# The norms of two phases applied by VectorE instead of ScalarE, with a new order of steps and a new table of banks

## The reference

```python
x = L0(x, ctx)    # rotary q and k; softmax attention over 256 keys; out projection; + x
def L1(x, c):     # mod = silu(c) @ ada_w + ada_b  -> shift, scale, gate for each half
    x0, x1 = x[:, :128], x[:, 128:]
    x0 = x0 + gate * mha(ln(x0) * (1 + scale) + shift)      # phase 1: each half attends to itself
    x1 = x1 + gate * mha(ln(x1) * (1 + scale) + shift)
    ...                                                     # phase 2: each half attends to the other
    ...                                                     # MLP: gelu(mod(ln(x)) @ fc1) @ fc2, gated
x = L2(x, ctx)    # phase 3: attention, + query, layer norm with gamma and beta
x = L3(x, ctx)    # phase 4: layer norm, attention with weights quantised to three values, + residual

def ln(x):
    mu = mean(x); var = mean((x - mu) ** 2)
    return (x - mu) / sqrt(var + eps)
```

## Time and profile before

| | |
|---|---|
| median of 3 runs | 300.79 us (299.94 to 304.99) |
| the profiled execution, own time | 301.38 us |
| its span, first to last instruction | 299.6 us |
| busy: TensorE, VectorE, ScalarE, GpSimd | 260.2, 241.9, 235.4, 173.8 us |
| mean granted TensorE clock | 0.978 of full speed |

### The profile page before, as it was taken

The page is one execution under the profiler, slowest core; times in us unless marked ns, Lnnn a source line. Parts: engine busy times, 40 slices in busy tenths (PEclk is TensorE's granted clock), DMA queues, the critical chain, the costliest instruction groups (busy, mean ns, idle before and its releaser), DMA issues.

```text
span 299.6 us, 8817 instructions
## 1 busy us (share of the span) xinstructions
PE 260.2 (87%) x3104; PEld 158.4 (53%) x3104; DVE 241.9 (81%) x561; ACT 235.4 (79%) x522; POOL 173.8 (58%) x274
## 2 busy tenths in 40 slices
PE   4275987899898888998888999999989999999983
PEld 3263543455565666666656766575444545445542
DVE  4179998999487897798889388998999999998912
ACT  1232456799998786598899998998989899898991
POOL 7778759347796667665482878856455654620000
PEclk9999799999999997899999999999999999999997
DMA  6678654211232232133231213212221213030001
GB/s 175 202 190 214 153 163 118 64 49 46 64 91 58 75 98 73 49 83 89 72 89 28 72 40 80 73 36 59 55 68 42 74 51 80 22 102 26 21 3 35
DMA packets 40619, 23.81 MB, mean 79 GB/s; under 512 B 4856, under 2 KB 39680, under 8 KB 40448
## 3 DMA queue, kind: packets, MB, share of 16 engines
q1 hardware_dynamic: 37264, 19.30, 24.7%
q10 hardware_dynamic: 3056, 3.83, 4.8%
q0 software_dynamic: 256, 0.13, 0.2%
HBM read 6.64 MB, written 0.54 MB: 24 GB/s over the span
## 4 chain that ended last, share of the span: by engine, by line
PE 45%; DVE 21%; DMA 9%; ACT 8%; SPq 7%; issue 7%; ACTq 1%; POOL 1%; DVEq 0%; POOLq 0%
PE ps L700 27%; DVE neg_max L1111 14%; PE ps_heads L700 13%; SPq L493 6%; DMA q_stack<-q_parts 5%; ACT probs L925 3%; DMA q_stack<-max_rows 2%; PE ps L875 2%; DMA rope_rows<-in_rope,pos_row 1%; PE ps L879 1%; SPq L574 1%; DVE stats L1071 1%; DMA pos_i<-in_pos 1%; ACTq L493 1%; ACT hidden L1043 1%
## 5 line engine op out<-in xcount | busy, mean ns | idle before, releaser
L1111 DVE TENSOR_REDUCE neg_max<-ps 128x2 f32<-128x512 f32 (+1 forms) x256 | 158.6, 682 | 9.4 <-PE ps L700 8.8
L925 ACT ACTIVATE probs<-ps 128x512 f32<-128x512 f32 x256 | 134.8, 626 | 10.4 <-PE ps L700 9.8
L700 PE MATMUL ps_heads<-probs,v_cols 128*32 128x256 f32 (+1 forms) x1280 | 76.9, 348 | 2.5 <-ACT probs L925 1.5
L700 PE MATMUL ps<-k_stack,q_stack 62*128 62x256 bf16 (+1 forms) x640 | 66.0, 255 | 5.9 <-DMA q_stack<-q_parts 5.1
L700 PE MATMUL ps<-q_stack,k_stack 64*128 64x256 bf16 (+1 forms) x640 | 66.0, 254 | 1.8 <-DMA q_stack<-max_rows 1.4
L700 PEld LDWEIGHTS ps<-k_stack,q_stack 62*128 62x128 bf16 x640 | 33.1, 96 | 28.1 <-issue 7.9
L700 PEld LDWEIGHTS ps<-q_stack,k_stack 64*128 64x128 bf16 x640 | 33.6, 96 | 24.3 <-issue 8.8
L700 PEld LDWEIGHTS ps_heads<-probs,v_cols 128*32 128x32 f32 x1280 | 31.9, 110 | 26.5 <-issue 11.1
L676 POOL TENSOR_TENSOR rstd<-var_eps,minus_half 128x2 f32<-128x2 f32 x20 | 14.1, 705 | 37.3 <-DVE var_eps L1077 37.3
L700 PE MATMUL ps<-src_t,w 128*128 128x256 f32 x96 | 29.6, 425 | 2.2 <-issue 1.1
L476 POOL TENSOR_TENSOR k_parts<-q_f,k_parts 128x256 bf16<-128x256 f32 x20 | 13.4, 669 | 28.6 <-issue 25.0
(11 more groups left out here) (117 smaller groups left out, 381.8 us busy)
## 6 DMA issues: line engine op xcount, KB each, us to landing
k_stack<-k_parts SPq DMA_DIRECT2D x120, 64.0 KB, 2.1
q_stack<-q_parts SPq DMA_DIRECT2D x114, 64.0 KB, 2.1
w<-in_w ACTq DMA_DIRECT2D x3, 512.0 KB, 5.0
gates<-gate_row SPq DMA_DIRECT2D x1, 1536.0 KB, 6.7
rows<-in_rows ACTq DMA_DIRECT2D x1, 704.0 KB, 4.8
w<-in_w ACTq DMA_DIRECT2D x1, 576.0 KB, 5.0
q_stack<-max_rows SPq DMA_DIRECT2D x36, 8.0 KB
ctx_t<-in_ctx_t SPq DMA_DIRECT2D x4, 128.0 KB, 2.5
```

Source lines behind the costliest of these rows:

```text
L700: return nc.tensor.matmul(out, lhs_t, rhs, start=start, stop=stop, **k)
L925: nc.scalar.activation(probs[:, n % PROB_BUFS, :], ps[bank[st]][:, :], ACT.Exp, scale=SCALE).then_inc(exped, 1)
L1111: nc.vector.tensor_reduce(dst, src, AX.X, ALU.max, negate=True).then_inc(max_taken, 1)
```

## The change

Three edits. First, `ON_DVE` gets the entries ("norm", 1) and ("norm", 2), so that the apply step of units 4 to 11 goes to VectorE. Second, VectorE gets code for it: for each of the two tiles one tensor_scalar, (x - mean) * rstd, with the mean from its own `mean_var` in place of GpSimd's `shift`. It still waits for `rstd_ready`, which GpSimd raises after `shift`, and for the transposes that read `normed` before. GpSimd's two instructions stay. Third, `ORDER` and `BANK_OF` are new strings.

```diff
 ON_DVE = (("max_split", 0), ("max_split", 1), ("max_split", 2), ("max_split", 3), ("max_split", 4),
-          ("max_t", 1), ("max_t", 4))
+          ("max_t", 1), ("max_t", 4),
+          ("norm", 1), ("norm", 2))
 ORDER = (
-    "HLHLLLLLRRPLRPDPSDHSDRDPSPGGRmmDmmLSPmmmHmmDXLRDPmTmDPGRmSmmmYmPmRXsmsPmSmssGTPmmsDmDvYvmssmsmmssmLDvmssDmmvssmXsvmmmm"
+    "HLLLLLHLRLRPLRPSPHSDDRDDPRPDGGmmmmmmSmmDmSmGRXmmLHmmPTRPPmDDmmXYmPsRGsmmmssTDPPsSsmDmmsvSvmYmmDsmsmssSmsDFmmXvvsmsssvm"
...
@@ scalar
-                elif st[0] == "apply":
+                elif st[0] == "apply" and not on_dve("norm", st[1]):
@@ vector
+                elif st[0] == "apply" and on_dve("norm", st[1]):
+                    u = st[1]
+                    dve.wait_ge(rstd_ready, no("norm", u, st[2]) + 1)
+                    if normed_before(u) is not None:
+                        dve.wait_ge(small_ready, no("small", "norm_t", normed_before(u)) + 1)
+                    for qt in range(NT):
+                        last = nc.vector.tensor_scalar(normed[:, qt, :], norm_source(u)[:, qt, :], mean_var[:, qt, 0:1],
+                                                       rstd[:, qt:qt + 1], ALU.subtract, ALU.mult)
+                    last.then_inc(applied, 1)
```

More of the change, by code:

```diff
@@ new lines @@
+    "vSNsvsmNsvvvXvvvNPODSDTOPPOSPmmmYsmsDsmDsNNvvssmDsSmvvmsNXvvvDvTPPOOPmmmOmmYssmssSsDvvSDNsssvNDmvmvvXvNvTOPSDmOmmYPOPs"
+    "ssNmDssmmvDNvmsvsmsvvNXvDSvvDOTYPOPDPmmOssmSmDssPsmmsvvSsNsmNSvmDvvvNvvDXOTMOmmmmMYmssDssOMmsNNMmmsPNXDvvvvvTssYMvDvvO"
+    "FMSOPPsDOssDMsNNFsmmmmNMvvmmsmPMmmvSvSvvmmmMmsmmmsDXMvvDTODPMPmYOmmPPSOsNmsssmmsNSPvsmsmvSNmDsssDmmMmmFDmmMvvsssmDXmsM"
+    "TvmssmmYmMvFvvPOssDmSmmsOPsmssOPmsmvNsmmmvNsDsNmDvssDmNvssXssmNmmvmSmTvNvYvNmOPSmmmsOssDmsOsssDsNmvvmsmmNvsmsmsXPDNvND"
@@ L154 @@
+    "ssvTsmsvYmmmNmNvvNPOssSmmPOmmmsPPOssssmsmSvNNmmDvsmsDmvXDssvssNNssDTvNmNmmDmmvvvNmOPmmSYDmsmOSsssOmsDssmvmsvsmmmDXNNss"
+    "sNNPvPvTNmmssmvYmNmsmvNmmSmsPsmvvsmSsDmDsDmPDOmmmssvssOvsXsssvTvYssOsmmsmmmvvssXvvsmsssmOsmTvvmXssmmsOvvTYYmssOsXsmmss"
+    "vvTsmsYsmvvXssssTsvvssssYOvvsssvsOvvvOOOO"
 )
 BANK_OF = (
[L159 to L160 removed]
@@ L165 @@
+    "3124506312542056432105624315062341562034125063415204613502461352046135024561302415630"
 )
```

22 lines of the change are left out of this document (7 added, 15 removed).

## The result

The changed kernel is slower: 307.69 us (median of 6 runs, 305.75 to 308.72) against 302.4 us (6 runs beside it). The ratio of the two is 1.022, with a 95% interval of 1.018 to 1.026. The profiled execution has a span of 306.9 us, against 299.6. The forecast was 299.4, with a range that ended at 303.5.

The account below looks back on a forecast made before the run. No single engine bounds throughout: VectorE early, SyncE's DMA queue at 100-160 us, ScalarE at 160-180, VectorE from about 175. A+B+C+D = -0.3-1.0-1.3+1.2 = -1.4 us, from 301.38 to 300.0, median 0.6 lower: 299.4 us, range 295.0 to 303.5.

Parts of the forecast that it names:

- A: Start of the new order: earlier maxima copy against two earlier weight loads, -0.3 us, bounds -1.1 and +2.1.
- B: Units 5 to 9: part of SyncE's 3.24 us wait between maxima removed, -1.0 us, bounds +1.2 and -4.5.
- the rest of the order: Remaining order and table of banks: same steps a few places up or down, 0, with 1.5 to either side.
- C: Norm removed from ScalarE, counted at units 8, 9 and 10 where it is full: -1.3 us, bounds 0 and -2.6.
- D: Norm added on VectorE, with its wait for rstd and one meeting with GpSimd: +1.2 us, bounds 0.5 and 2.5.
- rival 4: At the start, early weight loads cost their full 2.1 us: 300.7 or so; sign, first reduce after 25.5; chance 0.07.
- rival 1: Clock slump after the thin stretch at 108 to 116 us goes: B -4.5, time 295.9 us; chance 0.18.
- 0.23 each, 0.45 a pair: Price in D of the new norm on VectorE, from a CAST row; eight pairs give 3.6 us more VectorE time.
- rival 3: New norms on VectorE stretched by GpSimd: 11 us more VectorE time, +6 where it bounds, 305 us; chance 0.13.
- "At nothing" up to 160 us: Norm on VectorE costed at nothing up to 160 us, as VectorE has 3 us in 20 free there.
- two to four reduces that wait behind it: Reduces behind the norm on VectorE up to 160 us, called covered while TensorE has banks; otherwise 0.45 each time.

Follow-up runs that it names:

- work alone: Before, norm left on ScalarE, with two more tensor_scalar without a reader on VectorE at each of the eight norm places: 306.28 us, ratio 1.012.
- Latency alone: Before, with the norm on ScalarE moved one or two exps later in its list for units 4 to 11: 307.64 us, ratio 1.021.
- The clean joint: The changed kernel with the old order and banks up to unit 3's first value product, about 80 us, the new order behind: 305.57 us, ratio 1.009.
- The kernel with the early loads: Before, with only ScalarE's three weight loads moved forward to where the changed kernel has them: 303.11 us, ratio 1.003.
- The control: Before, with twelve pairs of neighbouring steps swapped, all of them steps of TensorE: 303.17 us, ratio 1.004.

## Why the prediction was wrong

**The step that weighs most is the order.** A, B and the rest of the order were forecast at -1.3 us together, with 1.5 to either side for the rest. The new order with the norm left on ScalarE measured +5.8 us (4.0 to 7.7). The norms, C and D, were forecast at -0.1; in the new order they measured about +1, not clear of noise, and in the old order +11 (3.6%), 2.1% for the later norm, which was a term at nothing, and 1.2% for the work.

**A, the start: -0.3 forecast, from -1.1 to +2.1.** Wrong in sign. By the means of the traces the new start costs 1.5 us at unit 3 (2.6 less 1.1), which is inside the range; by its runs the kernel with the old start came out some 4 us under the changed one, which is outside. The first reduce came 1.2 us later, at 25.39, short of rival 4's sign of 25.5 and within the spread of before's own start, so rival 4 is not shown. I worked out two places of the start (a copy that moves up, two loads that move forward) and let the rest of it stand at nothing. Behind the start, between units 4 and 5, is a place that I left out too, where the maxima meet a gate fold of GpSimd and steps of the quantiser; it is there in every trace with the new order. The 1.91 us hole near 51 is gone (the next wait of TensorE for q_stack is 0.92, at 57.96), and it gave nothing, for the reduces of unit 2 began 1.3 us later all the same. What makes the 4 us was not found: that cause stays open.

**B, units 5 to 9: -1.0 forecast.** About right in size, by another cause. From unit 6 to unit 10 the changed kernel goes from +3.4 to +2.5. The maxima leave SyncE's queue 9.9 us apart

```profile
117.41 1.37 SPq L575 DMA_DIRECT2D q_stack<-max_rows  x2
...
127.35 1.37 SPq L575 DMA_DIRECT2D q_stack<-max_rows  x2
```

where it had been 12.35, and the clock is full. But this is not the cause that I named alone: it contains the slump, whose value I put at 3.0 in rival 1 and which is 1.6 to 1.9 by unit 10 in the traces (last section), while 0.7 to 1.0 us are lost there beside it, where the new waits before the transposes are. So that the number came out near -1.0 is luck.

**C, ScalarE relieved: -1.3 forecast.** Nothing of it came. The wait before unit 10's turn

```profile
171.86 0.72 DVE L1125 STREAM_TRANSPOSE heads_raw<-ps_heads 128x512 f32<-128x512 f32 x1 [2.69 <-PE ps_heads L701]
...
178.46 0.65 DVE L1143 TENSOR_SCALAR normed<-x,mean_var,rstd 128x128 f32<-128x128 f32 x2
179.03 3.07 DVE L1112 TENSOR_REDUCE neg_max<-ps 128x2 f32<-128x512 f32 x5
```

is 2.69 us in place of 3.76, but the turn itself is at 171.86, 3.4 us later than 168.45, and from unit 10 to unit 12 another 1.8 us is lost. ScalarE is free of the norm and waits for the transposes in its place: 6.4 us behind them in all, against 0.4 (of this, 4.2 stand also in the trace of the new order with the norm on ScalarE). This is the step that failed as an idea: I subtracted the pair from ScalarE's list and never asked when the result would be there for the next phase.

**D, the norm on VectorE: +1.2 forecast, 0.5 to 2.5.** The step that failed is "0.23 each, 0.45 a pair", taken from a CAST without scalars; it measured 333 to 393 ns for six of the sixteen and 0.66 to 0.83 us for the ten that waited for GpSimd, 9.7 us in all where 3.6 had been worked out. Rival 3 had the mechanism ("VectorE stretched by GpSimd") with 11 us on top of the 3.6, too much, and was given 0.13. BN_STATS, which was never stretched (296 at most in this trace too), was the wrong witness for tensor_scalar. Each of the ten ended 80 to 83 ns after an instruction of GpSimd, as the pair of unit 4 does above. Yet as a cause of this kernel's time D is small, since in the new order the norm's place is worth about 1 us; that it is rival 3's mechanism does not make rival 3 right. The rule of the Trainium skill that I had set beside it (GPSIMD Engine Reference, Specifications) was the better witness. The trace agrees with it for GpSimd's two-input instructions; beside its TENSOR_SCALAR, with one tensor, no norm was stretched (0.33 to 0.39 us).

**"At nothing" up to 160 us.** By work it cost some 1.5 us there (work alone, above). By latency it was not costed at all: the "two to four reduces that wait behind it" were named, and those that stand ahead of it were called hidden. Latency alone is 2.1% in the old order. The new order avoids this by putting the norm sooner: a pair ends on average 1.86 us after rstd, as before (1.78), against 3.0 in the old order; this is the mean over the eight pairs of the time from rstd's end.

**The sum.** Of the 2.2%, the norm left on ScalarE gives 1.9 to the order and 0.3 to the norms. The clean joint gives 1.3 to the start of the new order and leaves 0.9 to the rest, and this rest holds the norms (3.3 to 3.6% in an order not made for them) less what the new order wins back. "The order alone is never neutral, 1.5 to either side" was the last term that should have been larger; the random swaps had 0.4%, an order searched anew had 1.9% with the norm on ScalarE.

## What to carry to other kernels

Before moving a small step to another engine, write down for both lists what stands between its operands and it, and who waits for its result: in the old order the latency of a 0.9 us step was worth more than its work (2.1% against 1.2%). Price an instruction by a row with the same operands; a tensor_scalar with two pointers is no CAST, and on VectorE beside a two-input instruction of GpSimd its price is what GpSimd has left to do. One pair of traces does not place a loss of 2 us: here kernels with the same instructions were up to 3.7 us apart at unit 3. And a re-searched order is a change of its own: split it off first, and at a place where both orders hold the same steps.

## What the runs showed of the hardware

A tensor_scalar on VectorE, f32 in SBUF with two [P, 1] scalars, took 333 ns for 128 columns and 286 to 292 for 32. So 96 columns cost some 45 ns, which is 2.1 elements in a ns, and the fixed part is 0.28 us; this part decided the size here. The Trainium skill (VectorE: DVE Perf Modes, the perf-mode tier table) gives two elements a cycle for it, with the 0.96 GHz of the same page an estimate of 1.9 in a ns, and the slope agrees within the few ns that the two medians are good for. Beside GpSimd's two-input instructions such an instruction ended 80 to 87 ns after GpSimd's, and took up to 1.13 us (the longest of the work alone); one of 32 columns up to 0.73.

What a slump of the clock costs: TensorE at 1.2 GHz. The kernel with the early loads has before's order from 100 us on, and no slump from 116 to 124 (clock 1.00; before 0.61):

```profile
116.00:124.00 8.00, 6.61 (x124) 4.39 (x121) 7.43 (x15) 5.41 (x15) 6.62 (x11) 1.00 0.30 77
```

Its last reduce of unit 7 starts 2.6 us ahead of before, the first 0.4 ahead, so within unit 7 the slump of 6.8 us cost 2.2 us. Not all of it stays: unit 8 starts 1.9 ahead, 1.5 won, and unit 10 2.3 ahead, 1.9 won. The control, without a slump there either, wins 1.5 and 1.6. The control has one of the same length earlier, from 50.2 to 57.0 us:

```profile
50.00:58.00 8.00, 6.61 (x56) 3.98 (x58) 4.61 (x8) 1.89 (x5) 4.06 (x5) 0.57 0.09 22
```

where before has none:

```profile
50.00:58.00 8.00, 6.10 (x73) 3.31 (x74) 6.85 (x14) 3.92 (x10) 4.71 (x6) 1.00 0.14 35
```

From unit 1 to unit 3 it went from 0.6 ahead to 2.0 behind, 2.6 us. The kernel with half the norms moved, which has before's instructions up to there, has a slump from 50.5 to 57.3 us and loses 2.7. A slump from 10.8 to 21.1 us went by with no loss (norm later on ScalarE, 0.6 us ahead at unit 0). Which stretches are hit differs between kernels that have the same instructions up to there, and the mean clock of a run tells little of its time: the changed kernel took 308.71 us at a mean of 0.989 and 308.72 at 0.951.
